# Column one-hots kept twice and read four times, eleven lanes on VectorE, seven on ScalarE, staged by GpSimd

## The reference

```python
edge_index = jnp.stack([src, dst])
x = _layernorm(x + _L0_gnn_ref(x, edge_index, ...), axis=-1)   # agg = segment_sum(h[src], dst)
x = _layernorm(x + _L1_gnn_ref(x, src, dst, edge_weight1, ...), axis=-1)
x = _layernorm(x + _L2_gnn_ref(x, node_vec1, edge_index, edge_weight, ...), axis=-1)
x = _layernorm(x + _L3_gnn_ref(x, L3_gnn_W, L3_gnn_bias, edge_index, 3125), axis=-1)
```

## Time and profile before

| what | value |
|---|---|
| median of 3 runs | 1645.76 us (1643.49 to 1646.26) |
| the profiled execution: time | 1645.85 us |
| its span, first to last instruction | 1644.1 us |
| mean granted TensorE clock, share of 2.4 GHz | 0.943 |
| PE busy over the span | 1414.9 us (86%) |
| DVE busy | 1246.3 us (76%) |
| ACT busy | 609.4 us (37%) |
| POOL busy | 44.4 us (3%) |
| the placing loop (third program block) | from 103.9 to about 207.4 us |

### The profile page before, as it was taken

One profiled execution on the slowest core, in us unless ns is written; L12 is line 12 of the kernel. 1 busy time (PEld: TensorE's weight loads), 2 busy tenths in 40 slices (PEclk: granted clock), 3 DMA queues, 4 the chain that ended last, 5 costly groups with the idle time before them and its releaser, 6 DMA issues. The chain is left out here.

```text
span 1644.1 us, 44005 instructions
## 1 busy us (share of the span) xinstructions
PE 1414.9 (86%) x16795; PEld 1304.8 (79%) x16795; DVE 1246.3 (76%) x3619; ACT 609.4 (37%) x1115; POOL 44.4 (3%) x64
## 2 busy tenths in 40 slices
PE   0745558878996999999999958689999999999997
PEld 0434446668995888888888838689999999999997
DVE  4899988874436888888888856668768777778776
ACT  0259959990103777777777730010000000000000
POOL 1100000000000000000000021000000000000000
PEclk9978779997998999999999969879999999999999
DMA  1000015542003545454323142000000000000000
GB/s 20 8 1 0 0 47 153 158 138 57 2 1 87 142 138 141 122 156 111 110 73 110 37 111 62 6 1 2 2 2 2 2 2 2 2 2 2 2 3 20
DMA packets 37008, 83.91 MB, mean 51 GB/s; under 512 B 22941, under 2 KB 23957, under 8 KB 36863
## 3 DMA queue, kind: packets, MB, share of 16 engines
q1 hardware_dynamic: 32231, 74.42, 15.9%
q10 hardware_dynamic: 4410, 7.43, 1.9%
q0 software_dynamic: 224, 0.13, 0.1%
HBM read 60.76 MB, written 21.14 MB: 50 GB/s over the span
## 5 line engine op out<-in xcount | busy, mean ns | idle before, releaser
L1751 PE MATMUL L_psA<-L_parts,mat 125*128 125x192 bf16 x6250 | 517.1, 246 | 0.0
L1751 PEld LDWEIGHTS L_psA<-L_parts,mat 125*128 125x128 bf16 x6250 | 515.5, 98 | 1.0 <-DVE L_parts L1828 0.8
L1181 PEld LDWEIGHTS L_ps_pre<-L_drow,mat 128*128 128x128 bf16 x2250 | 129.1, 98 | 30.3 <-issue 1.1
L1690 ACT COPY L_wk<-L_Wk 128x64 f32 (+1 forms) x10 | 2.0, 242 | 391.9 <-PE L_psA L1751 391.9
L1815 DVE TENSOR_REDUCE L_sumr<-L_psA 125x64 f32<-125x192 f32 x225 | 80.5, 358 | 70.9 <-PE L_psA L1751 70.4
L1181 PE MATMUL L_ps_pre<-L_drow,mat 128*128 128x32 bf16 (+3 forms) x2250 | 133.4, 213 | 0.0
L681 PE MATMUL ps_count<-onehot 128*128 128x125 bf16 x1200 | 106.9, 218 | 17.0 <-DVE onehot L644 9.5
L1370 DVE TENSOR_TENSOR L_e<-L_e,mat 128x512 f32<-128x512 f32 x125 | 86.1, 689 | 39.3 <-ACT L_e L1268 39.3
L644 DVE TENSOR_TENSOR onehot<-iota_bf,codes 128x1024 bf16<-128x1024 bf16 x150 | 100.6, 687 | 18.3 <-PE ps_count L681 17.3
L774 PE MATMUL L_psA<-L_gparts,mat 125*128 125x192 bf16 x1250 | 110.3, 250 | 4.5 <-DVE L_gparts L787 4.5
L774 PEld LDWEIGHTS L_psA<-L_gparts,mat 125*128 125x128 bf16 x1250 | 106.8, 101 | 5.2 <-DVE L_gparts L787 4.9
(11 more groups left out here) (306 smaller groups left out, 2316.4 us busy)
## 6 DMA issues: line engine op xcount, KB each, us to landing
L_drow<-rows_d SPq DMA_DIRECT2D x25, 728.0 KB
mat<-rows_d SPq DMA_DIRECT2D x25, 640.0 KB, 4.3
mat<-m_d SPq DMA_DIRECT2D x16, 684.2 KB
m_d<-panel SPq DMA_DIRECT2D x13, 684.2 KB
m_d<-xb SPq DMA_DIRECT2D x12, 684.2 KB
mat<-m_d ACTq DMA_DIRECT2D x9, 684.2 KB
L_drow<-rows_d SPq DMA_DIRECT2D x25, 84.5 KB
mat<-m_d SPq DMA_DIRECT2D x16, 79.4 KB
```

What stands on the lines that cost most here:

```text
L1181: last = nc.tensor.matmul(ps_pre[bank][:, to:to + n], w, drow[k][:, of:of + n], start=False, stop=(r == 2 and cc == pieces[-1][0]))
L1751: last = nc.tensor.matmul(ps[:, 0:3 * D], t.mat[0:B, kb, b * B:b * B + P], parts[src][:, kb].rearrange("p r d -> p (r d)"), start=(kb == 0 ...
```

## The change

`col4` and `slots4` become `col2` and `slots2` with two copies, `iotac` and `ohc` keep each value twice. The multiplication into `rows` reads each pair of `ohc` twice by a dimension with step zero, so it still writes 1872 values. The split of the slot one-hots moves from 9 + 9 lanes to 11 on DVE and 7 on ACT. The copy of ACT's slots into `stage` moves from DVE to a new GpSimd loop.

```diff
-        iotac = sb("iotac", [P, NC, DUP], BF16)
+        iotac = sb("iotac", [P, NC, 2], BF16)
...
-                spread4 = lambda ap: flat(ap).unsqueeze(2).broadcast_to([P, NB * W, DUP])
-                D1(nc.vector.scalar_tensor_tensor(col4[:].rearrange("p b j t -> p (b j) t"), spread4(col), 1.0,
-                                                  spread4(sblk), ALU.add, ALU.add))
+                twice = lambda ap: flat(ap).unsqueeze(2).broadcast_to([P, NB * W, 2])
+                D1(nc.vector.scalar_tensor_tensor(col2[:].rearrange("p b j t -> p (b j) t"), twice(col), 1.0,
+                                                  twice(sblk), ALU.add, ALU.add))
...
-        HOT = W // 2
+        HOT = 11
...
-        ohc = sb("ohc", [P, 2, W, NC, DUP], BF16)
+        ohc = sb("ohc", [P, 2, W, NC, 2], BF16)
...
                     dve.wait_ge(win_used, b + 1)
-                    nc.vector.tensor_copy(stage[:, k, :], slot[:, bass.ds(b, 1), HOT:W].rearrange("p o j -> p (o j)")
-                                          ).then_inc(stage_set, 1)
                     nc.vector.tensor_tensor(
-                        ohc[:, k], window(col4, b).unsqueeze(2).broadcast_to([P, W, NC, DUP]),
-                        iotac[:].unsqueeze(1).broadcast_to([P, W, NC, DUP]), ALU.is_equal).then_inc(ohc_ready, 1)
-                    by4 = [P, HOT, P // DUP, DUP]
+                        ohc[:, k], window(col2, b).unsqueeze(2).broadcast_to([P, W, NC, 2]),
+                        iotac[:].unsqueeze(1).broadcast_to([P, W, NC, 2]), ALU.is_equal).then_inc(ohc_ready, 1)
+                    by2 = [P, HOT, P // 2, 2]
...
                     dve.wait_ge(ohc_ready, b + 1)
+                    by5 = [P, W, NC, 2, 2]
                     for q in range(REC // DUP):
                         last = nc.vector.tensor_tensor(
-                            rows[:, k, q].rearrange("p j (c t) -> p j c t", t=DUP), ohc[:, k],
-                            window(rec, b)[:, :, q * DUP:(q + 1) * DUP].unsqueeze(2).broadcast_to([P, W, NC, DUP]),
-                            ALU.mult)
+                            rows[:, k, q].rearrange("p j (c u t) -> p j c u t", u=2, t=2),
+                            ohc[:, k].unsqueeze(3).broadcast_to(by5),
+                            window(rec, b)[:, :, q * DUP:(q + 1) * DUP].rearrange("p j (u t) -> p j u t", t=2).unsqueeze(2
+                                                                            ).broadcast_to(by5), ALU.mult)
...
+            @block.gpsimd
+            def _(pool):
+
+                def body(b, k):
+                    pool.wait_ge(win_used, b + 1)
+                    nc.gpsimd.tensor_copy(stage[:, k, :], slot[:, bass.ds(b, 1), HOT:W].rearrange("p o j -> p (o j)")
+                                          ).then_inc(stage_set, 1)
+                in_pairs(pool, NB, body)
```

More of the change, by code:

```diff
@@ L141, in _ @@
                                allow_small_or_imprecise_dtypes=True)
-                nc.gpsimd.iota(iotac[:], [[1, NC], [0, DUP]], base=1, channel_multiplier=0,
+                nc.gpsimd.iota(iotac[:], [[1, NC], [0, 2]], base=1, channel_multiplier=0,
                                allow_small_or_imprecise_dtypes=True).then_inc(consts, 1)
@@ L194, in place_edges @@
         col = sb("col", [P, NB, W], F32)
-        slots4, col4 = (sb(n, [P, NB, W, DUP], BF16) for n in ("slots4", "col4"))
+        slots2, col2 = (sb(n, [P, NB, W, 2], BF16) for n in ("slots2", "col2"))
         rec = sb("rec", [P, NB, W, REC], BF16)
@@ L371, in _ @@
                 act.wait_ge(slotted, 1)
-                nc.scalar.copy(slots4[:].rearrange("p b j t -> p (b j) t"),
-                               slot[:].rearrange("p b j -> p (b j)").unsqueeze(2).broadcast_to([P, NB * W, DUP]))
+                nc.scalar.copy(slots2[:].rearrange("p b j t -> p (b j) t"),
+                               slot[:].rearrange("p b j -> p (b j)").unsqueeze(2).broadcast_to([P, NB * W, 2]))
                 act.wait_ge(counted2, 1)
                 nc.scalar.copy(c.placed_i[:], ps_cnt[0:1, 0:1])
-        HOT = W // 2
+        HOT = 11
         ohr = sb("ohr", [P, 2, W, P], BF16)
         away = sb("away", [P, W - HOT, P], BF16)
-        ohc = sb("ohc", [P, 2, W, NC, DUP], BF16)
+        ohc = sb("ohc", [P, 2, W, NC, 2], BF16)
         rows = sb("rows", [P, 2, REC // DUP, W, NC * DUP], BF16)
@@ L391, in body @@
                     dve.wait_ge(win_used, b + 1)
-                    nc.vector.tensor_copy(stage[:, k, :], slot[:, bass.ds(b, 1), HOT:W].rearrange("p o j -> p (o j)")
-                                          ).then_inc(stage_set, 1)
                     nc.vector.tensor_tensor(
-                        ohc[:, k], window(col4, b).unsqueeze(2).broadcast_to([P, W, NC, DUP]),
-                        iotac[:].unsqueeze(1).broadcast_to([P, W, NC, DUP]), ALU.is_equal).then_inc(ohc_ready, 1)
-                    by4 = [P, HOT, P // DUP, DUP]
+                        ohc[:, k], window(col2, b).unsqueeze(2).broadcast_to([P, W, NC, 2]),
+                        iotac[:].unsqueeze(1).broadcast_to([P, W, NC, 2]), ALU.is_equal).then_inc(ohc_ready, 1)
+                    by2 = [P, HOT, P // 2, 2]
                     nc.vector.tensor_tensor(
-                        ohr[:, k, 0:HOT, :].rearrange("p j (n t) -> p j n t", t=DUP),
-                        c.iota1_bf[:].rearrange("p (n t) -> p n t", t=DUP).unsqueeze(1).broadcast_to(by4),
-                        window(slots4, b)[:, 0:HOT, :].unsqueeze(2).broadcast_to(by4), ALU.is_equal)
+                        ohr[:, k, 0:HOT, :].rearrange("p j (n t) -> p j n t", t=2),
+                        c.iota1_bf[:].rearrange("p (n t) -> p n t", t=2).unsqueeze(1).broadcast_to(by2),
+                        window(slots2, b)[:, 0:HOT, :].unsqueeze(2).broadcast_to(by2), ALU.is_equal)
                     dve.wait_ge(ohc_ready, b + 1)
+                    by5 = [P, W, NC, 2, 2]
                     for q in range(REC // DUP):
                         last = nc.vector.tensor_tensor(
-                            rows[:, k, q].rearrange("p j (c t) -> p j c t", t=DUP), ohc[:, k],
-                            window(rec, b)[:, :, q * DUP:(q + 1) * DUP].unsqueeze(2).broadcast_to([P, W, NC, DUP]),
-                            ALU.mult)
+                            rows[:, k, q].rearrange("p j (c u t) -> p j c u t", u=2, t=2),
+                            ohc[:, k].unsqueeze(3).broadcast_to(by5),
+                            window(rec, b)[:, :, q * DUP:(q + 1) * DUP].rearrange("p j (u t) -> p j u t", t=2).unsqueeze(2
+                                                                            ).broadcast_to(by5), ALU.mult)
                     last.then_inc(dve_ready, 1)
```

## The result

The changed kernel takes 1627.55 us (1627.16 to 1631.54, 4 runs) against 1645.47 us before: ratio 0.9899, 95% interval 0.9887 to 0.9911, or 14.6 to 18.6 us less by the interval. The forecast was 1632.5 us, range 1627 to 1641.

A forecast was written before the change was run, and what follows sets the result against it. ACT was taken to bound the placing loop at 4.05 us a window. Savings of 0.93 us at setup, 0.62 at the first window and 11.8 over 24 windows, together 13.3, gave 1632.5 us from 1645.85, range 1627 to 1641.

The forecast's parts named there:

- The bound and its successor: Placing loop: ACT sets the pace at 4.05 us a window, DVE is next at 3.88.
- DVE's window: Placing loop: after the change DVE's copy, compares and products sum to 3.44 us a window, if the zero step costs nothing.
- The rule of adjacent words: Products in the loop: full rate only for adjacent 4-byte words; would add 1.26 us a window, time about 1662.
- ACT's window: Placing loop: with seven lanes and a smaller relu ACT's period is 3.27 us, below DVE's by 0.17 us.
- POOL's copy: Placing loop: the seven-element copy takes 0.14 us and costs DVE 0.10 us a window.
- PE at the low clock: Placing loop: PE's matmuls at low clock delay DVE by 0.04 us in 11 of 24 windows, 0.02 a window.
- The start: Loop start to first matmul: 3.62 us instead of 4.24, 0.62 us less.
- The zero step: Rival: re-reading pairs slows the products to one element per step, 5.56 us a window, 1680.5 us; chance 0.08.
- the long hold: Rival: POOL's copy holds DVE for 1.4 us, window 4.86 us, time 1663.7 us; chance 0.04.
- The late copy: Rival: POOL's copy waits for a DVE product, 3.9 us in some 9 windows, 1635.6 up to 1641 us; chance 0.12.
- a sign of being wrong: Loop: a POOL copy far above 0.2 us was among the trace signs that would show the prediction wrong.
- The extreme: Rival: POOL's copy gets no turn until DVE stands still, 9.2 us a window, 1768 us; chance 0.02.

The follow-up runs named there:

- e2: The changed kernel with nine slot lanes on VectorE and nine on ScalarE again: 1645.57 us, ratio 1.0005.
- e3: The changed kernel with the column one-hots kept four times, as before the change: 1640.71 us, ratio 0.9967.
- e7: The changed kernel with the column one-hots kept once and read four times by a zero step in the innermost dimension: 1680.05 us, one run.
- e10: The changed kernel with ten lanes on VectorE and eight on ScalarE: 1637.95 us, one run.
- e4: The changed kernel with GpSimd's copy writing the seven slots 64 times over, 448 elements instead of 7: 1635.76 us, one run.
- e6: The changed kernel with GpSimd's copy writing the seven slots 32 times over, 224 elements instead of 7: 1632.88 us, one run.
- e1: The changed kernel with ScalarE's slots copied by VectorE again instead of GpSimd: 1631.2 us, ratio 0.9913.
- e5: The changed kernel measured once more, unchanged: 1627.37 us, ratio 0.9892.
- e11: The changed kernel with twelve lanes on VectorE and six on ScalarE: 1637.48 us, one run.
- e9: The kernel before with only the lanes split eleven to seven, four copies and VectorE's copy of the slots kept: 1643.18 us, ratio 0.9991.

## Why the prediction was right

- **The bound and its successor.** ACT at 4.05, then DVE: shown by e2 (4.07 with nine lanes) and e3 (3.92 with four copies).
- **DVE's window.** The sum of starts was 3.44; 3.44 is what the trace has. Slope, `ohc`, slots and the free zero step all held, and e7 shows where it would not have held. The rule of adjacent words in the Trainium skill ("Vector Engine (DVE) Microarchitecture Reference", section 5.2) would by the prediction's estimate have added 1.26 us a window if a word read twice counted as a hop. It doesn't count as one here: the product kept its 1.12 us.
- **ACT's window.** 3.27 was computed; where ACT waits for nothing the changed kernel has 3.25. Behind DVE's window it is covered. In e10 the windows in which nothing is late are 3.65 or 3.71 us, against 3.66 computed.
- **POOL's copy, the term that was mis-sized.** I gave 0.10 us a window, 2.4 us, to "DVE waits for most of a copy of 0.14". It is the other way round: POOL's copy takes 0.44 us because it waits for DVE's product, and DVE is held only for what the copy reads, 0.8 ns an element in e4 and e6, by estimate 0.006 us for seven. The right term was nothing (e1). That the two exclude each other is what the Trainium skill says ("SBUF — State Buffer", "Who interferes with whom"); e4 agrees, with a product of 1.48 us in place of 1.12.
- **PE at the low clock**, 0.02 us a window, 0.5 us in all: paid once, at about 0.4. DVE's third window starts at 108.17, 3.83 us behind its second, because PE's first window still ran at the low clock (granted 0.56 up to 108.2) and ended late. From there on the granted clock is 1.00 to the end, so it was not paid again; over the loop it was 0.96 after, 0.79 before.
- **The start.** 0.62 was forecast, 0.3 came: POOL's first copy took 0.7 us, not 0.14, since it ended only behind DVE's first compare.
- **What is left.** The terms that runs bear out are 14.5 + 0.9 + 0.3 = 15.7 us, against 13.3 in the sum; the difference is in the main POOL's term. That makes 1630.1. The medians give 17.9 us (result) and 17.8 (e5). The last 2.2 us come from no term of the prediction: its range holds 1627.55 only because the spread of the runs was added at the lower end, and by 0.55 us, which is luck in part. Where they come from is not settled. In the first pair of profiles it is the clock of the rank stage, in e5 the work behind the loop, 3.9 us shorter; both differ between executions, and 15.7 us is a ratio of 0.9905, inside both intervals.
- **The rivals.** The zero step and the long hold did not come. The late copy did in part: 0.44 us in most windows is far above the 0.2 that the prediction had named as a sign of being wrong. It cost nothing, since ACT's lanes wait only 0.09 us behind it and PE waits for DVE's product, not for ACT. The extreme that I gave 0.02, POOL without a turn until DVE stands still, exists: one copy in the loop of e7 and one in e11, of 7 to 12 us, and none in the nine other profiles with POOL's copy.

## What to carry to other kernels

Where two engines are nearly level, price both windows with the change in: each half here was worth nothing that could be measured alone (e2, e9), both 18 us. Starts in the trace, not durations, add up to the period to the hundredth. A small copy given to GpSimd was free for VectorE's two-input instructions but comes when they let it; give it slack, and expect an execution now and then in which it waits for many of them (2 of 11 profiles here).

## What the runs showed of the hardware

- A GpSimd copy and VectorE's two-input products and compares exclude each other: the copy holds VectorE for 0.17 us with 224 elements and 0.36 with 448. GpSimd's copy itself mostly ends some 0.05 us behind the running VectorE instruction. In two profiles it waited through eight of them, 7.18 and 11.97 us. What decides that is open.
- A product whose one input reads each bf16 pair twice and then the next took 1.12 us for 1872 elements, as long as with four stored copies; with each element read four times in the innermost dimension it took 2.10.
- Matmuls that read runs of four bf16 values took 1.82 us for 18, against 1.78.
